# A gated long-convolution stage with mixture-of-experts behind it: kernel rows split once, all nine product rows summed on TensorE, the kv remainder on GpSimd

## The reference

```
kv  = einsum('bhil,bhjl->bijhl', ctx, ctx)
y   = causal convolution of kv with ssm_kernel[h] along l      (by FFT in the reference)
out = y + kv * D[h]
out = einsum('bijhl,bhil->bjhl', out, q)
x   = x + tanh(g_xattn) * out
```

## Time and profile before

| | |
|---|---|
| median of 3 runs | 830.31 us (830.1 to 832.09) |
| profiled execution, its own time | 832.62 us |
| its span, first to last instruction | 830.8 us |
| mean granted TensorE clock | 0.970 |
| busy share of the span: PE, PEld, DVE, ACT, POOL | 91%, 85%, 79%, 54%, 46% |
| first stage | about 14 to 289 us |
| chain that ended last, largest parts | PE L1198 29%, PE L1223 16%, DVE L760 9%, PE L1135 5% |

### The profile page before, as it was taken

One profiled execution on the slowest core, in us unless ns is written; L12 is line 12 of the kernel. 1 busy time (PEld: TensorE's weight loads), 2 busy tenths in 40 slices (PEclk: granted clock), 3 DMA queues, 4 the chain that ended last, 5 costly groups with the idle time before them and its releaser, 6 DMA issues.

```text
span 830.8 us, 15761 instructions
## 1 busy us (share of the span) xinstructions
PE 756.1 (91%) x4730; PEld 708.6 (85%) x4730; DVE 657.3 (79%) x1167; ACT 444.6 (54%) x594; POOL 382.4 (46%) x206
## 2 busy tenths in 40 slices
PE   3888887787889999999999999989999999999994
PEld 3887787787888889999999999979989989899993
DVE  7999999999999854684258958866986885896891
ACT  5333344343343233221258958766876875895882
POOL 5767657667567001451123443534444344554242
PEclk9999899999889999999999999999999999999997
DMA  6334544334442213121724668767656665443200
GB/s 231 123 122 137 169 153 135 133 121 158 159 141 77 90 64 52 32 45 26 266 51 134 168 168 236 190 197 180 183 168 149 196 170 162 102 80 63 53 14 0
DMA packets 43027, 105.86 MB, mean 127 GB/s; under 512 B 7121, under 2 KB 7121, under 8 KB 42961
## 3 DMA queue, kind: packets, MB, share of 16 engines
q1 hardware_dynamic: 30128, 80.15, 28.4%
q0 software_dynamic: 12832, 24.93, 15.6%
HBM read 148.87 MB, written 29.18 MB: 214 GB/s over the span
## 4 chain that ended last, share of the span: by engine, by line
PE 58%; DVE 24%; issue 7%; DMA 4%; ACT 2%; SPq 1%; ACTq 1%; DVEq 0%; POOL 0%; POOLq 0%
PE bank L1198 29%; PE bank L1223 16%; DVE prod L760 9%; PE bank L1135 5%; DVE prod L750 3%; DVE prod L753 3%; PE bank L1145 3%; PE bank L1206 3%; DMA raw<-in_weights 2%; PE bank L1095 2%; DVE st L697 2%; DMA out<-ys,slot_info 2%; DVE prod L756 1%; DVE kv_lo L766 1%; ACT w_hi L663 1%
## 5 line engine op out<-in xcount | busy, mean ns | idle before, releaser
L1068 DVE TENSOR_TENSOR w_lo<-raw,w_hi 128x1408 fp32r<-128x1408 f32 x94 | 148.8, 1621 | 45.9 <-ACT w_hi L656 45.8
L1334 POOL DMA_INDIRECT out<-ys,slot_info x47 | 87.1, 1853 | 101.0 <-DMA out<-ys,slot_info 58.0
L1323 POOL DMA_INDIRECT tn<-t_rows,slot_info x47 | 71.2, 1516 | 131.9 <-DVE tT_lo L808 120.3
L656 ACT ACTIVATE w_hi<-raw 128x1408 fp32r x94 | 125.0, 1375 | 7.4 <-DMA raw<-in_weights 5.5
L760 DVE TENSOR_TENSOR prod<-prod 128x256 f32<-128x256 f32 x64 | 108.3, 1692 | 0.0
L1135 PE MATMUL bank<-kv_hi,toep_hi 128*128 128x288 f32 x320 | 105.7, 330 | 2.3 <-DVE toep_lo L380 2.3
L1077 DVE TENSOR_TENSOR hid<-hid,bank 128x352 f32<-128x352 f32 x79 | 40.7, 515 | 81.6 <-ACT hid L670 81.6
L1135 PE MATMUL bank<-kv_hi,toep_lo 128*128 128x288 f32 x320 | 100.0, 313 | 0.0
L1135 PE MATMUL bank<-kv_lo,toep_hi 128*128 128x288 f32 x320 | 99.8, 312 | 0.0
L670 ACT ACTIVATE hid<-bank 128x352 f32<-128x352 f32 x79 | 36.0, 456 | 115.9 <-PE bank L1198 115.9
L1073 DVE TENSOR_TENSOR w_lo<-raw,w_hi 128x1536 fp32r<-128x1536 f32 x47 | 82.4, 1752 | 17.6 <-ACT w_hi L663 17.6
(11 more groups left out here) (184 smaller groups left out, 1861.0 us busy)
## 6 DMA issues: line engine op xcount, KB each, us to landing
raw<-in_weights SPq DMA_DIRECT2D x94, 704.0 KB
raw<-in_weights SPq DMA_DIRECT2D x47, 768.0 KB
toep<-kpad SPq DMA_DIRECT2D x16, 512.0 KB, 4.5
cx<-in_ctx SPq DMA_DIRECT2D x16, 384.0 KB, 3.2
stage<-in_weights SPq DMA_DIRECT2D x16, 272.0 KB, 2.7
xt<-in_x SPq DMA_DIRECT2D x16, 256.0 KB, 4.5
xr<-in_x SPq DMA_DIRECT2D x16, 256.0 KB, 2.7
out<-x SPq DMA_DIRECT2D x16, 256.0 KB, 2.1
```

The lines of the kernel that those rows point to most:

```text
L656: act.activation(w_hi[s % 2][:, a:b], raw[:, bass.ds(half + a, b - a)], ACT.Copy).then_inc(hi_ok[n_], 1)
L1068: dve.tensor_tensor(w_lo[s % 2][:, a:b], raw[:, bass.ds(half + a, b - a)], w_hi[s % 2][:, a:b].bitcast(F32), ALU.subtract).then_inc(lo_ok[ ...
L1323: pool.indirect_dma_start(out=tn[o % 2][:], out_offset=None, in_=t_rows, in_offset=bass.IndirectOffsetOnAxis(ap=slot_info[:, 3 * i:3 * i + ...
L1334: pool.indirect_dma_start(out=out, out_offset=bass.IndirectOffsetOnAxis(ap=rows, axis=0), in_=ys[o % 2][:], in_offset=None, bounds_check=R ...
```

## The change

It has four parts. (1) The kernel rows are split into a high and a low part once, at the start, as 32 x 640 rows; both go to DRAM, and each tile loads two Toeplitz matrices, hi and lo, into `toep_hi` and `toep_lo`. `toep` and the two splits a tile are gone; SP loads the Toeplitz rows of tile t + 2 at the end of its turn t, behind a wait for the convolution of tile t. (2) The DVE sum of L760 is gone, and PE sums nine rows a block in place of seven. (3) kv_lo is DVE's for tile 0 only, as before; from tile 1 on GpSimd subtracts all 2304 columns. (4) The PSUM banks of the convolution are named as two pairs of 1024 columns, and two SBUF buffers (xt, xn) change places with `toep`; no work hangs on it. The second half is left as it is, written out without loops.

```diff
-ROWS_LEFT = (2, 3, 4, 5, 6, 7, 8)
-PROD_STEPS = 7
+PROD_STEPS = 6
...
-        kpad = nc.dram_tensor("kpad", (HEADS, 640), F32, kind="Internal").ap()
+        kpad = [nc.dram_tensor(f"kpad_{n}", (HEADS, 640), F32, kind="Internal").ap() for n in ("hi", "lo")]
...
-        toeplitz = bass.AP(kpad.tensor, 0, [[2 * 640, TILES], [1, P], [640, 2], [1, L]])
+        toeplitz = [bass.AP(k.tensor, 0, [[2 * 640, TILES], [1, P], [640, 2], [1, L]]) for k in kpad]
...
         def form(eng, t):
             p = t.odd
-            wait(eng, kvl_ok, t)
             wait(eng, kvl2_ok, t)
+            if t.within(1, 2):
+                eng.wait_ge(kvl_ok, 1)
...
         def _(sp):
...
-            sp.wait_ge(kpad_ok, 1)
-            sp.dma_start(kpad, krow[:]).then_inc(kpad_out, 16)
-            sp.wait_ge(kpad_out, 16)
+            sp.wait_ge(krowh_ok, 1)
+            sp.dma_start(kpad[0], krow_hi[:].bitcast(F32)).then_inc(kpad_out, 16)
+            sp.wait_ge(krowl_ok, 1)
+            sp.dma_start(kpad[1], krow_lo[:].bitcast(F32)).then_inc(kpad_out, 16)
+            sp.wait_ge(kpad_out, 32)
...
                 if which == "toep":
-                    sp.dma_start(toep[p][:].rearrange("p (h c) -> p h c", h=2),
-                                 toeplitz[bass.ds(t.v, 1)].rearrange("x p h c -> (x p) h c")).then_inc(toep_in[p], 16)
+                    for part, rows in ((toep_hi, toeplitz[0]), (toep_lo, toeplitz[1])):
+                        sp.dma_start(part[p][:].bitcast(F32).rearrange("p (h c) -> p h c", h=2),
+                                     rows[bass.ds(t.v, 1)].rearrange("x p h c -> (x p) h c")).then_inc(toep_in[p], 16)
...
             def turn(t):
                 first, ahead = t.within(0, 1), not t.within(TILES - 2, TILES)
                 if ahead:
                     wait(sp, kv_ok, (t + 1) * 2)
                     load(t + 2, "ctx")
-                    wait(sp, toepl_ok, t + 1)
-                    load(t + 2, "toep")
                     wait(sp, xn_ok, t + 1)
                     load(t + 2, "x")
...
                 if not first:
                     store(t - 1, "t")
                     store(t - 1, "tT")
+                if ahead:
+                    wait(sp, conv_ok, (t + 1) * 8)
+                    load(t + 2, "toep")
...
-            def split_toep_hi(t):
-                p = t.odd
-                wait(act, conv_ok, (t - 1) * 8)
-                wait(act, toep_in[p], (t.half() + 1) * 16)
-                act.activation(toep_hi[p][:], toep[p][:], ACT.Copy).then_inc(toeph_ok, 1)
...
+            act.wait_ge(kpad_ok, 1)
+            act.activation(krow_hi[:], krow[:], ACT.Copy).then_inc(krowh_ok, 1)
             split_kv_hi(At(0))
             std_x(At(0))
             norm_x(At(0))
-            split_toep_hi(At(0))
             q_copy(At(0))
...
             dve.tensor_tensor(krow[:, P - 1:P], krow[:, P - 1:P], drow[:], ALU.add).then_inc(kpad_ok, 1)
+            dve.wait_ge(krowh_ok, 1)
+            dve.tensor_tensor(krow_lo[:], krow[:], krow_hi[:].bitcast(F32), ALU.subtract).then_inc(krowl_ok, 1)
...
             def products(t, lb):
...
-                wait(dve, prod_ok, (t * 4 + lb) * PROD_STEPS + 5)
-                dve.tensor_tensor(prod[par][:, 5 * P:7 * P], prod[par][:, 0:2 * P], prod[par][:, 5 * P:7 * P],
-                                  ALU.add).then_inc(prod_ok, 1)
...
                 products(t, 2)
                 if not last:
                     scale_x(t + 1)
-                    split_kv(t + 1)
                 products(t, 3)
...
             def conv(t, lb):
...
-                            wait(pe, toepl_ok, t + 1)
-                            wait(pe, kvl_ok, t + 1)
+                            wait(pe, toep_in[p], (t.half() + 1) * 32)
+                            if t.within(0, 1):
+                                pe.wait_ge(kvl_ok, 1)
                             wait(pe, kvl2_ok, t + 1)
...
             def sum_rows(t, lb):
...
-                for r in ROWS_LEFT:
+                for r in range(PRODROWS):
                     mm = pe.matmul(ps_o[:, lb * P:(lb + 1) * P], prod[lb % 2][:, r * P:(r + 1) * P], ident[:],
-                                   is_transpose=True, start=(r == ROWS_LEFT[0]), stop=(r == ROWS_LEFT[-1]))
+                                   is_transpose=True, start=(r == 0), stop=(r == PRODROWS - 1))
...
             def split_kv(t):
                 wait(pool, kvh_ok, t + 1)
-                pool.tensor_tensor(kv_lo[t.odd][:, KV_DVE:], kv[:, KV_DVE:], kv_hi[t.odd][:, KV_DVE:].bitcast(F32),
+                a = KV_DVE if t.within(0, 1) else 0
+                pool.tensor_tensor(kv_lo[t.odd][:, a:], kv[:, a:], kv_hi[t.odd][:, a:].bitcast(F32),
                                    ALU.subtract).then_inc(kvl2_ok, 1)
...
             def turn(t):
                 if not t.within(TILES - 1, TILES):
                     form(pool, t + 1)
                 split_shared(t)
-                if t.within(0, 1):
-                    pool.wait_ge(conv_ok, 1)
                 if not t.within(TILES - 1, TILES):
-                    split_toep(pool, t + 1)
                     split_kv(t + 1)
```

More of the change, by code:

```diff
@@ L170, in program @@
         out_t = out.rearrange("(t p) l -> t p l", p=P)
-        bank = [ctx.enter_context(nc.psum_tensor(f"bank{n}", [P, 512], F32)) for n in range(8)]
-        ps_conv = [[bank[0], bank[1]], [bank[2], bank[3]]]
+        ps_conv = [ctx.enter_context(nc.psum_tensor(f"pair{n}", [P, 1024], F32)) for n in range(2)]
+        bank = [ps_conv[n // 2][:, n % 2 * 512:n % 2 * 512 + 512] for n in range(4)]
+        bank += [ctx.enter_context(nc.psum_tensor(f"bank{n}", [P, 512], F32))[:] for n in range(4, 8)]
         ps_o, ps_q, ps_t, ps_gate = bank[4], bank[5], bank[6], bank[7]
@@ L196, in program @@
         cx = sb2("cx", [P, BLOCKS * GROUPS * EXT], F32, one)
-        toep = sb2("toep", [P, 2 * L], F32, one)
+        xt = sb2("xt", [P, L], F32, one)
+        xn = sb2("xn", [P, L], F32, one)
         stage = sb2("stage", [P, STAGE], F32, one)
@@ L208, in program @@
         kv_lo = sb2("kv_lo", [P, BLOCKS * GROUPS * PAIRS], F32R, one)
-        xt = sb2("xt", [P, L], F32, one)
         xr = sb2("xr", [P, L], F32, one)
-        xn = sb2("xn", [P, L], F32, one)
         q = sb2("q", [P, BLOCKS * GROUPS * EXT], F32, one)
@@ L214, in program @@
         krow = sb("krow", [HEADS, 640], F32, one)
+        krow_hi, krow_lo = sb("krow_hi", [HEADS, 640], F32R, one), sb("krow_lo", [HEADS, 640], F32R, one)
         drow = sb("drow", [HEADS, 1], F32, one)
@@ L273, in program @@
         kvh_ok, kvl_ok, kvl2_ok = sem("kvh_ok"), sem("kvl_ok"), sem("kvl2_ok")
-        toeph_ok, toepl_ok = sem("toeph_ok"), sem("toepl_ok")
+        krowh_ok, krowl_ok = sem("krowh_ok"), sem("krowl_ok")
         conv_ok, prod_ok, summed = sem("conv_ok"), sem("prod_ok"), sem("summed")
@@ L374, in form @@
                               ALU.mult).then_inc(kv_ok, 1)
-        def split_toep(eng, t):
-            p = t.odd
-            wait(eng, toeph_ok, t + 1)
-            eng.tensor_tensor(toep_lo[p][:], toep[p][:], toep_hi[p][:].bitcast(F32), ALU.subtract).then_inc(toepl_ok, 1)
         def h_bank(n):
@@ L480, in _ @@
             sp.wait_ge(kv_ok, 2 * TILES)
-            sp.wait_ge(toepl_ok, TILES)
+            sp.wait_ge(xn_ok, TILES)
             for p in (0, 1):
@@ L606, in turn @@
                 if not t.within(TILES - 1, TILES):
-                    split_toep_hi(t + 1)
                     split_kv_hi(t + 1)
@@ L740, in products @@
                 for h in range(2):
-                    y = ps_conv[par][h][:]
+                    y = ps_conv[par][:, h * 512:h * 512 + 512]
                     qo = lb * GROUPS * EXT + h * BATCH
@@ L758, in products, with split_first_kv @@
                                       view(qq, qo + 4 * G, [[4 * G, 2], [G, 4], [1, BATCH]]), ALU.mult).then_inc(prod_ok, 1)
-                wait(dve, prod_ok, (t * 4 + lb) * PROD_STEPS + 5)
-                dve.tensor_tensor(prod[par][:, 5 * P:7 * P], prod[par][:, 0:2 * P], prod[par][:, 5 * P:7 * P],
-                                  ALU.add).then_inc(prod_ok, 1)
-            def split_kv(t):
-                wait(dve, kvh_ok, t + 1)
-                dve.tensor_tensor(kv_lo[t.odd][:, 0:KV_DVE], kv[:, 0:KV_DVE], kv_hi[t.odd][:, 0:KV_DVE].bitcast(F32),
+            def split_first_kv():
+                dve.wait_ge(kvh_ok, 1)
+                dve.tensor_tensor(kv_lo[0][:, 0:KV_DVE], kv[:, 0:KV_DVE], kv_hi[0][:, 0:KV_DVE].bitcast(F32),
                                   ALU.subtract).then_inc(kvl_ok, 1)
@@ L778, in _ @@
             dve.memset(prod[1][:], 0.0).then_inc(setup_dve, 1)
-            split_kv(At(0))
-            split_toep(dve, At(0))
+            split_first_kv()
             dve.wait_ge(gate_tanh, 1)
@@ L1134, in conv @@
                         for m, (w, z) in enumerate(((toep_hi, kv_hi), (toep_hi, kv_lo), (toep_lo, kv_hi))):
```

(2 more changed lines are left out.)

## The result

The changed kernel takes 778.07 us (median of 4 runs, 775.36 to 778.33) against 830.96 us for the kernel before on the same chip: a ratio of 0.9355, with a 95% interval of 0.933 to 0.938. The forecast was 784 us, with a range of 779 to 799. The profiled execution took 778.33 us with a span of 776.5, 54.3 us less than before (830.8 of span).

The account below looks back on a forecast made before the run. DVE was taken as the bound through line 760's waits for GpSimd, PE as the next; 14 x (14.1 - 17.53) = -48.0, + 0.5 + 1.1 = -46.4 us, from the median 830.31 to 784 us, range 779 to 799.

Parts of the forecast that it names:

- Step 1: DVE, first stage: without line 760 and its kv_lo from tile 1 on, 8.6 us a turn, no longer the bound.
- Step 2: PE, first stage: with nine rows a turn takes 13.87 us plus 0.2 for loop branch and waits, 14.1 us.
- Step 3: GpSimd: kv_lo of 2304 columns takes 5.4 us, between 5.15 and 5.85; its work is 12.0 us a turn.
- Step 4: Chain from residual through kv_hi and GpSimd's kv_lo to PE: about 1 us of slack, so longer kv_lo costs nothing.
- Step 5: Toeplitz rows split once, a second 512 KB load a turn: lands in time, cost taken as nothing.
- Step 6: Start, up to turn 1: +0.5 us, bounds -0.5 and +2.7.
- Step 7: End, last turn of the first stage: five sums gain two matmuls each, +1.1 us.
- The first rival: GpSimd's chain becomes the bound, the residual being held by form: 14.5 to 15.8 us a turn, 790 to 808 us; chance 0.20.
- The clock rival: PE's granted clock stays at 0.93 in the first stage: turns of 15.1 us, 798 us; chance 0.12.
- The second half: Everything after 289 us, untouched by the diff: must still take 541.8 us.

Follow-up runs that it names:

- a_rows_only: The kernel before with only line 760 removed and PE summing nine rows; Toeplitz split and shared kv_lo as before: 776.66 us, ratio 0.9349.
- d_add_back: The changed kernel with line 760 back on DVE and seven rows summed on PE: 829.15 us, ratio 0.9981.
- h_kv_shared: The changed kernel with kv_lo shared again, DVE 1280 columns and GpSimd 1024: 777.48 us, ratio 0.9377.
- f_seven_no_add: The changed kernel with rows 0 and 1 of the products left out of the sum, added by nobody: 773.23 us, ratio 0.9288.
- l_gate_later_plus544: The changed kernel with an extra 1.43 us GpSimd instruction a turn ahead of kv_lo, and PE's last sum before the gate: 785.42 us, ratio 0.9455.
- g_start_order: The changed kernel with ctx of tile 1 and the shared weights' first stage loaded ahead of the four Toeplitz loads: 777.67 us, ratio 0.9354.
- b_kv_only: The kernel before with only kv_lo from tile 1 on given whole to GpSimd; line 760 and Toeplitz split stay: 869.83 us, ratio 1.0477.

## Why the prediction was right and where it was wrong

- *Step 1, line 760.* Right, and stronger than said: it alone carries the gain (a_rows_only), and putting it back takes all of it away (d_add_back). DVE's part of kv_lo, which the step took off with it, was worth nothing (h_kv_shared). The 8.6 us a turn left for DVE are too few: it is busy 130.3 us in 40 to 230, 9.3 us a turn, which costs nothing.
- *Step 2, PE's turn.* **This is the term that failed.** It was put at 14.1 us and measured 13.62, which over 14 turns is 6.7 us. From turn 1's convolution to turn 15's, as in the table, 14 turns took 190.1 us, 13.58 each, and the difference is 7.5 us. It has two errors, both on the same side. The 0.2 us for the loop's branch and waits were not there: the pieces join without a gap across turns in the loop. And 12.55 us of the last turn contained a wait: the gate's 1.03 us in the earlier trace rows were 0.81 of work and 0.22 of waiting for tT. Without both the sum would be 13.68 us. To add the price of eight matmuls, 0.88 us, to a duration that holds a wait is to count a part twice, since the new matmuls stand where the wait was. f_seven_no_add shows it backwards: eight matmuls less gave 0.66. My lower bound of 13.87 us, "PE with nobody in its way", was no lower bound.
- *Step 3, kv_lo on GpSimd.* 5.15 us, the lower of the three estimates, the one by the slope of two instructions of the same kind; 5.4 in proportion was 5% too high.
- *Step 4, the slack.* 1.05 us was said, 0.68 measured. Right that it costs nothing; the ring through the buffer kv (l_gate_later_plus544) was missed, and it doesn't bind here.
- *Step 5, the Toeplitz loads.* Right that they cost nothing in steady turns: the second load of a tile landed in 5.3 to 9.9 us, and PE never waited for it. In the start the queue is longer and later. Two of the four Toeplitz loads stand ahead of ctx of tile 1, which is issued at 9.73 us (6.58 before), and all four ahead of the shared weights, at 13.30 (9.09 before). Form waited until 18.07 us and shared_hi until 22.86, the two waits here:

```profile
18.07 4.33 POOL L368 TENSOR_TENSOR kv<-cx 128x2048 f32<-128x2048 f32 x1 [3.90 <-DMA cx<-in_ctx]
...
22.86 0.66 ACT L586 ACTIVATE shared_hi<-stage 128x544 fp32r<-128x544 f32 x1 [7.51 <-DMA stage<-in_weights]
```

- *Step 6, the start.* +2.8 us, not +0.5; just above the step's upper bound. The two delays of tile 0 came as worked out: form started at 7.0 and kv_lo ended at 15.5. But PE begins turn 0 right behind that, 1.5 us later than before, and is busy with it until 29.33, which the step didn't count: 1.3 us of the 2.8. The other 1.5 are PE's wait until 30.84 for kv_lo of tile 1, made by the loads above; g_start_order took that wait away.
- *Step 7.* +0.6 for +1.1, the same hidden wait: the last turn has two gates, 1.03 and 1.04 us before, 0.81 and 0.83 after.
- *The first rival.* Excluded. The residual ran beside form in 14 of its 16 turns and without it in the last two, and took between 745 and 751 ns in all of them, timelines of DVE and GpSimd:

```profile
128.29 0.75 DVE L715 SCALAR_TENSOR_TENSOR x<-bank,small,xr 128x512 f32<-128x512 f32 x1 [0.68 <-PE bank L1135]
...
124.64 4.33 POOL L368 TENSOR_TENSOR kv<-cx 128x2048 f32<-128x2048 f32 x1
```

  The sentence of the Trainium skill (SBUF — State Buffer, Who interferes with whom) that one SBUF input outside the two-port modes doesn't contend holds here with a pointer scalar in SBUF besides. What the same section lists of tensor_scalar, on conditions for its operands that the prediction left out, does not show for this 128x1 form: L725 ran at 131.72 beside shared_lo (131.12 to 132.49) and took 0.21 us again. Its main rule is that a VectorE instruction with two SBUF inputs and a GpSimd one that reads SBUF exclude each other, and that the second to start waits for the whole of the first. b_kv_only shows this with 4.99 us behind 5.11.
- *The clock rival.* Excluded: the granted clock was 1.00 from 14 to 240 us, with PE busy for 223.1 of the 226. Turned round it came true in b_kv_only, at 0.80.
- *The second half.* 2.2 us shorter in the profiled spans, which I had at zero. But the other runs, f_seven_no_add apart, had 538.8 to 543.3 us there, with the same code and a granted clock of 0.99, so that both 542.6 and 540.5 lie inside the spread. The 2.2 us are not shown to come from the change. As much of the miss may be chance, which is more than the 0.9 us by which the time lies outside the range.

The sum of these errors, -7.5 + 2.3 - 0.5 - 2.2 = -7.9 us, is what separates -46.4 from -54.3. The start's error partly hid that of the turn. The range was built from a lower bound on the turn that wasn't one.

## What to carry to other kernels

In this kernel a DVE tensor_tensor with both inputs in SBUF cost its own 0.41 us and what was left of GpSimd's instruction at that moment, 4.99 us in all behind one of 5.11. Look for such an instruction on the engine that sets the pace before counting elements, and don't lengthen GpSimd's instructions while it is still there. When work is added to an engine that will be the bound, take its pieces from a stretch without waits and look at each against its other occurrences, since a wait in the sample is covered by the new work and would be counted twice. And a change of several parts should be run part by part: here one part was the whole gain, one was a loss of 4.8% alone, and the third, worth 3% alone, only paid for the second once the first was in.

## What was unexpected

- A part that removes 1.5 us a turn from the busiest engine made the kernel 39 us slower (b_kv_only), through a blocked sum of 4.99 us and a granted clock of 0.80.
- GpSimd is held up too, though little: in the kernel with line 760 the short instruction of form took 915 ns on average and toep_lo 2587, without it 742 and 2405 (a_rows_only).
- Summing nine rows in place of seven cost PE less than the eight matmuls' own price, 0.66 for 0.88 us a turn.
